# Mixture of experts over sorted token and choice pairs, in place of every expert over every token

## The reference

```python
xn = _layernorm(x)                                # (2, 1024, 128), float32
for i in range(4):                                # the transformer: 16 heads of 8
    x1 = x1 + mha(layer_norm(x1), causal mask + alibi)
    x1 = x1 + gelu(layer_norm(x1) @ ffn1.T + b) @ ffn2.T + b      # 128 -> 512 -> 128
x1 = layer_norm(x1)

logits = xf @ router_w + router_b                 # the mixture: 2048 tokens, 8 experts
top_w, sel = jax.lax.top_k(logits, 2)
gates = softmax(top_w)
for i in range(8):
    h = gelu(xf @ w1[i] + b1[i])                  # 128 -> 512
    acc += (h @ w2[i] + b2[i]) * sum(gates * (sel == i))
return x + x1 + acc
```

## Time and profile before

| | us |
|---|---|
| median of three runs | 1606.52 |
| profiled execution | 1611.84 |
| its span | 1610.0 |
| TensorE busy | 1391.6 (86% of the span) |
| VectorE busy | 1046.6 (65%) |
| ScalarE busy | 999.9 (62%) |
| GpSimd busy | 220.1 (14%) |

### The profile page before, as it was taken

One profiled execution on the slowest core, in us unless ns is written; L12 is line 12 of the kernel. 1 busy time (PEld: TensorE's weight loads), 2 busy tenths in 40 slices (PEclk: granted clock), 3 DMA queues, 4 the chain that ended last, 5 costly groups with the idle time before them and its releaser, 6 DMA issues.

```text
span 1610.0 us, 36678 instructions
## 1 busy us (share of the span) xinstructions
PE 1391.6 (86%) x12960; PEld 710.0 (44%) x12960; DVE 1046.6 (65%) x2259; ACT 999.9 (62%) x1214; POOL 220.1 (14%) x399
## 2 busy tenths in 40 slices
PE   3789898899889998798988998799998989889974
PEld 2444344454435344353443544344444535444343
DVE  5657666776676765666677766567667766676625
ACT  2055776568666775557865686565866577656841
POOL 4001200121010300112001210013001120011001
PEclk9579999999999999899999999899999999999997
DMA  5111313103021311203120130301211031201010
GB/s 184 56 29 32 97 32 99 30 30 105 24 74 32 96 32 46 75 26 97 32 74 30 30 110 20 99 17 60 82 46 58 19 97 31 78 30 31 5 47 13
DMA packets 82666, 88.87 MB, mean 55 GB/s; under 512 B 8744, under 2 KB 76080, under 8 KB 82480
## 3 DMA queue, kind: packets, MB, share of 16 engines
q1 hardware_dynamic: 82480, 86.43, 17.7%
HBM read 54.15 MB, written 33.55 MB: 54 GB/s over the span
## 4 chain that ended last, share of the span: by engine, by line
PE 67%; DVE 14%; issue 7%; ACT 7%; DMA 2%; SPq 2%; DVEq 0%; POOL 0%; ACTq 0%
PE PS L775 16%; PE PS L740 13%; PE PS L700 12%; PE PS L691 10%; DVE mx L996 7%; PE PS L757 4%; PE PS L721 2%; PE PS L745 2%; ACT PR L586 2%; PE PS L763 2%; DMA x<-orec 1%; DVE hb L920 1%; ACT hb L568 1%; PE PS L725 1%; DVE st L889 1%
## 5 line engine op out<-in xcount | busy, mean ns | idle before, releaser
L996 DVE TENSOR_REDUCE mx<-PS 128x1 f32<-128x512 f32 (+3 forms) x1280 | 773.1, 633 | 354.9 <-PE PS L745 204.1
L586 ACT ACTIVATE PR<-PS 128x1024 f32<-128x1024 f32 (+3 forms) x768 | 610.7, 808 | 441.0 <-PE PS L763 248.1
L740 PE MATMUL PS<-Kop,Qop 64*128 64x512 bf16 (+3 forms) x1536 | 415.5, 341 | 105.0 <-DVE mx L996 93.1
L757 PE MATMUL PS<-Qop,Kop 64*128 64x512 bf16 (+3 forms) x1536 | 368.3, 335 | 19.3 <-ACT PR L586 17.7
L740 PEld LDWEIGHTS PS<-Kop,Qop 64*128 64x128 bf16 x1536 | 128.4, 94 | 557.7 <-DVE mx L996 419.0
L775 PE MATMUL PS<-PR,vbuf 128*32 128x512 f32 (+3 forms) x3072 | 335.0, 509 | 0.4 <-ACT PR L586 0.4
L700 PE MATMUL PS<-wE,hb 128*128 128x128 f32 x1536 | 204.9, 284 | 14.6 <-ACT mrow L558 4.7
L700 PEld LDWEIGHTS PS<-wE,hb 128*128 128x128 f32 x1536 | 182.1, 193 | 33.6 <-issue 14.4
L745 PE MATMUL PS<-idb,mk 64*128 64x64 bf16 x2048 | 196.0, 193 | 0.0
L745 PEld LDWEIGHTS PS<-idb,mk 64*128 64x128 bf16 x2048 | 166.7, 97 | 40.7 <-issue 5.9
L763 PE MATMUL PS<-idb,mk 64*128 64x64 bf16 x2048 | 180.4, 191 | 0.0
(11 more groups left out here) (76 smaller groups left out, 940.6 us busy)
## 6 DMA issues: line engine op xcount, KB each, us to landing
Qop<-qst SPq DMA_DIRECT2D x64, 256.0 KB, 2.9
Kop<-kst SPq DMA_DIRECT2D x64, 256.0 KB, 3.2
kst<-parts SPq DMA_DIRECT2D x32, 256.0 KB, 3.0
qst<-parts SPq DMA_DIRECT2D x16, 384.0 KB, 2.8
wE<-in_moe SPq DMA_DIRECT2D x8, 514.0 KB, 3.6
kst<-parts SPq DMA_DIRECT2D x32, 128.0 KB, 2.8
qst<-parts SPq DMA_DIRECT2D x16, 256.0 KB, 2.9
Qop<-mrow SPq DMA_DIRECT2D x256, 3.0 KB
```

The lines of the kernel that those rows point to most:

```text
L586: act.activation(PR[:, c % 4, :, 0:n], PS[:, 2 * (c % 2):2 * (c % 2) + 2, 0:n], ACT.Exp)\
L740: last = pe.matmul(PS[:, 5 + k % 2, n * e:n * e + n], Qop[r, par, a, P * i:P * i + P], Kop[r, kb, a, 512 * c:512 * c + n], start=True, sto ...
L757: last = pe.matmul(PS[:, 2 * (c % 2) + j, 0:n], Kop[r, kb, a, P * kt:P * kt + P], Qop[r, par, a, q0:q0 + n], start=True, stop=not DIAG[t])
L996: dve.tensor_reduce(mx[:, par, i, 2 * heads[0] + j:2 * heads[-1] + j + 1:2, c], PS[:, 5 + k % 2, 0:n * len(heads)].rearrange("p (h n) -> p ...
```

## The change

The 4096 (token, choice) pairs are sorted by expert on the chip. Each expert's pairs fill whole tiles of 128 rows, 40 tiles in all (the most that eight experts can need), and four tiles are a group, so there are ten groups in place of 32 expert chunks.

- Before phase 0 TensorE counts, with two products of 128 x 256, how many earlier pairs go to the same expert; VectorE makes of it each pair's row (`slot`) and each tile's expert (`expert_of`), in 17 small operations spread over the first unit's first pass (`routing`). The dense gates, their transposes and the product with the second bias go. SP clears `xs` in DRAM with a DMA of 2.6 MB.
- GpSimd writes the normalised tokens into `xs` with 32 indirect DMAs of 128 rows (`scatter`): 8 and 8 in unit 0 of phase 0 and 16 in unit 1.
- For each group SP reads four expert numbers from SBUF into a register and issues nine DMAs (`group_in`): four times the expert's weights (514 KB each) and bias, and the group's rows. Before, eight DMAs of 514 KB did for the whole kernel. There is one buffer for a group.
- A group is turned (`xt`, new, four transposes), has four `h` pieces (piece f is tile f: four products of 128 x 128 with that tile's expert), a gelu and a `y`. VectorE adds the biases (for `h` with a 128 x 512 operation per piece), and SP writes the result to `ys`.
- Groups lie in unit 3 of phases 0 to 6 and in unit 2 of phases 1, 3 and 5. Unit 0 of every phase has no expert work any more, nor has unit 2 of phases 0, 2, 4, 6 and 7. All `h` of the X chunks go through ScalarE; before, VectorE did them.
- In phase 7 GpSimd gathers the rows back from `ys` with 32 indirect DMAs (16 in unit 0, 16 in unit 1), and in unit 2 multiplies by the gates and adds, in 16 operations of 128 x 512 (`combine`). The last step of the output (`final`) has three operations in place of four.

```diff
-CHUNKS = (("E", 0), ("X", 0), ("X", 1), ("E", 1), ("E", 2), ("E", 3))
-GELUS = ((0, 10), (0, 22), (1, 7), (2, 10), (2, 17), (3, 10))
+CHUNKS = (("X", 0), ("X", 1), ("E", 0), ("E", 1))
+GELUS = ((0, 22), (1, 7), (2, 11), (3, 11))
+XT_AT = {2: (2, 3), 3: (3, 3)}
...
+            def group_in(g):
+                for i in range(GROUP):
+                    e = sp.value_load(expert_of[0:1, ds(GROUP * g + i, 1)], min_val=0, max_val=E - 1)
+                    sp.dma_start(wG[:, i, :], moe[ds(e, 1), :, :].rearrange("l p n -> (l p) n")).then_inc(S["c_g"], 16)
+                    sp.dma_start(bG[:, i, :], rb_b2[ds(e + 1, 1), :].to_broadcast([P, D])).then_inc(S["c_g"], 16)
+                sp.dma_start(xG[:, :, :], xsv[ds(g, 1), :, :, :].rearrange("g p t d -> (g p) t d")).then_inc(S["c_g"], 16)
...
+                            if half == 0 and j == 2 and f is not None and b == 1:
+                                group_out(group_of(2, b, f), base + number(contents, "y", 2) + 1)
+                                group_in(group_of(3, b, f))
...
+            def scatter(first, last):
+                for k in range(first, last):
+                    pool.indirect_dma_start(out=xs[:, :], out_offset=bass.IndirectOffsetOnAxis(ap=slot[:, k:k + 1], axis=0),
+                                            in_=xe[:, k % NT, :], in_offset=None).then_inc(S["c_xs"], 16)
+            def gather(first, last):
+                for k in range(first, last):
+                    pool.indirect_dma_start(out=both[:, k // NT, k % NT, :], out_offset=None, in_=ys[:, :],
+                                            in_offset=bass.IndirectOffsetOnAxis(ap=slot[:, k:k + 1], axis=0))\
+                        .then_inc(S["c_both"], 16)
...
+                    for m in range(FT):
+                        last = pe.matmul(PS[:, bank, P * m:P * m + P], wG[:, f, P * m:P * m + P], xGT[:, P * f:P * f + P],
+                                         start=True, stop=True)
```

More of the change, by code:

```diff
@@ L172, in build @@
         rb = sb("rb", [P, E])
-        b2e = sb("b2e", [E, D])
+        tri = sb("tri", [P, P])
+        ones = sb("ones", [P, 2 * P])
+        zero = sb("zero", [P, P])
+        bound = sb("bound", [P, RANKS])
+        place = sb("place", [P, TILES])
         finw = sb("finw", [P, 2, D])
@@ L240, in build @@
         S = {n: sem(n) for n in names}
-        c_wE = [sem(f"c_wE{i}") for i in range(2)]
         c_ldl = [sem(f"c_ldl{i}") for i in range(2)]
@@ L782, in phase @@
                 row = 1 - b
-                place = f if b == 1 else q
-                g0 = 0 if f is None else gelus_before(p)
-                done = [k for k in range(6) if CHUNKS[k][0] == "E" or f is not None]
+                g0 = gelus_before(b, f)
+                done = chunks_of(b, f, q)
                 for j in range(PH):
@@ L957, in v_out, with out_of_bank @@
                                   ALU.add).then_inc(S["s_taken"], 1)
-            def out_of_bank(n, kind, which, p, biases, b, row, bank=7):
+            def out_of_bank(n, kind, which, g, biases, b, row, bank=7):
                 if kind == "h":
@@ L963, in out_of_bank @@
                 if kind == "y":
-                    y_out(n, which, p, biases, row, bank)
+                    y_out(n, which, g, biases, row, bank)
                 if kind == "wo":
@@ L1004, in maximum, with ln_step @@
                         .then_inc(S["s_negm"], 1)
-            def ln_step(idx, row, c, first, now, ready):
+            def ln_step(idx, row, c, first, now, ready, src=xr):
                 (j, k), (j0, s0) = now, first
```

407 lines of the change are left out of this document (262 added, 145 removed).

## The result

The changed kernel took 1615.85 us in the median of eight runs (1610.41 to 1619.11), the kernel before, run beside it, 1609.12. The ratio is 1.0042 with a 95% interval of 1.0022 to 1.0059: 0.4% slower, where 1550 us were predicted. The profiled execution took 1610.41 us, the one of before 1611.84; what follows compares these two, so it explains a difference of -1.4 us; by the medians it is +6.7, since the profiled execution of the changed kernel was the fastest of its eight runs.

A forecast was written before the change was run, and what follows sets the result against it. TensorE was taken to bound units with expert or transformer work, the loop of first pass and maxima the others. Savings of -116, plus GpSimd 28, SP 2 and clock 30, gave -56 us: 1550 us median, range 1515 to 1590, eight in ten 1482 to 1612.

The forecast's parts named there:

- Empty units: Six units left without expert work: 30.5 us each, five from about 41.5, unit 0 of phase 0 from 43.7; -66 us.
- Units with a group: Ten units holding an expert group: 40.4 us each, from 42.2 (seven units 3) or 41.5 (three units 2); -15 us.
- the price of a group: In each of ten units: 0.9 x 9.3 us of TensorE work on 30.5, and 1.5 for the uncovered gelu; 40.4 us.
- the term of 2 us for the groups' weights: SP loading the second group's weights in phases 1, 3, 5: 2 us in all, 15 at worst; TensorE waiting would disprove it.
- The clock: TensorE's clock halves behind 17 bare gelus, 3.8 us each: 30 us in all, bounds none and 110 us.
- Unit 0 of phases 1 to 7: Expert h ahead of the DRAM chain's end was free; only the gelu behind is saved, 2.5 of 4.5 us counted; -17 us.
- Unit 1: Half a y less in slot 0, partly covered by the X chunk's gelu: 1 us each, 2 in phase 0; -9 us.
- GpSimd: Indirect DMAs of scatter and gather make other engines wait: 28 us together, 2 us at t = 0.65, 77 at 2.13.
- t: Time one indirect DMA holds GpSimd: taken as 1.27 us, between bounds of 0.65 and 2.13.
- the stall in unit 0 of phase 7: Gather's DMAs ahead of rstd make VectorE wait in the layer norm: 20.3 - 13.7 = 6.6 us.
- rival 3: Slower, by GpSimd: its 64 indirect DMAs eat the 116 us gain at t = 2.3; 1653 us at 3.1; chance 0.12.
- rival 2: Everything is given back: clock at 60 us, GpSimd at 45, groups late by 10; 1605 us; chance 0.12.

## Why the prediction was wrong, step by step

- **Empty units: right.** 30.5 us was forecast from the stretch of the earlier trace rows; the five take 30.2 to 30.9, four of them at full clock throughout. -57 for -55. VectorE is busy for 78% of one (23.91 of 30.50 us), where over 80% was foretold.
- **Units with a group: the largest failure, 33 us.** Three terms were too small. The first is the price of a group: the model (0.9 us for each us of TensorE, 1.5 for the bare gelu) gave 40.4 us; an undisturbed one takes 41.6, so 12 us for ten. The slots show where: over an empty unit turning takes 1.6 us (0.7 in the model), the gelu 2.3 (1.5), `h` and `y` 3.5 and 3.8 (7.7 together). The second is the term of 2 us for the groups' weights, "15 at worst": the load was taken as 8 us at 326 GB/s, and ten slots, 13 us, as enough for it. It took 13.6 to 14.6 us. In phases 1, 3 and 5 TensorE waits 3.1 to 4.1 us for it, which the prediction had named as a sign that it was wrong, and then runs cold; moving the group gave 19 us in all, 15.6 in those three units. The third is the clock: 18 us were put into these units, and the extra matmuls took back 25.5, of which a part belongs to the loop's turn. How the 33 us divide among the three is not shown more closely than that.
- **The clock: right mechanism, size too small.** All 17 gelus leave TensorE idle, and behind 14 of them the clock falls (all seven of the X chunks, seven of the ten groups). 30 us were forecast, 39 were to be had behind the gelus, and 12 more behind the wait in unit 0, which the prediction had not counted at all. By its own terms: the extra matmuls took away 81 us at half clock in the units concerned, 4.8 us for each gelu where 3.8 were taken, and 35.3 us of time with it, 0.44 us for each where 0.48 were taken.
- **Unit 0 of phases 1 to 7: wrong, 19 us.** The prediction said that `h` lay beside the chain through DRAM, and that the gelu lay behind it and its 4.5 us would go, of which I counted 2.5. That step failed. The gelu did begin behind the normalise step in phases 2, 4 and 6, and ahead of it in the others; but with this work gone the normalise step starts within 0.7 us of where it did, and taking the work away alone cost 7 us. What the prediction left out is what stood in its place: the longer wait, and a clock at half for 40 us more, though it charged the clock for the 17 gelus alone.
- **Unit 1: right in sum.** +14.9 for +14: in phase 7 the gather made 9.1 of it (10.7 were forecast), in the others the fall behind the X chunk's gelu ate the shorter slot 0.
- **GpSimd: right, with luck in t.** It was taken as 1.27 us, the middle between bounds of 0.65 and 2.13, and is 1.25; nothing in the rows of before spoke for the middle. Spreading the DMAs gave 19 us against 28 forecast; the stall in unit 0 of phase 7 (6.6 us) did not show, since VectorE's wait lay there already. So rival 3, with t at 2.3 us or more, is out. The Trainium skill, "SBUF — State Buffer", section "SBUF: two separate sides", gives 3100 ns for a DMA from GpSimd beside a copy on VectorE. That did not come about here: with VectorE's maxima going on beside it, 5.2 us in the 20 us of the second half of the scatter, a DMA holds GpSimd for 1.25 us. No run shows the condition that the page names.
- **Rivals.** The outcome is rival 2, all given back, with its price of 1605 us and its causes in the main: the clock at 51 us (39 and 12; it had 60), GpSimd at 19 (45), late groups at 19 (10). It had 0.12, and the forecast 0.56, because the five sure units were set against it; they held, and the rest gave back as much. (The chance of slower, rival 3 and a quarter of rival 2, comes to 0.15 and not 0.14.)

One step was missing altogether: the loop's turn, some 6 us more than before by one execution of each kernel.

## What to carry to other kernels

When work is taken off an engine that was nearly always busy, look at each place where it goes for the wait that the work had covered: the wait stays, and the clock of TensorE falls in it. Work beside a wait or close behind it has no price of its own; what it is worth is read from a kernel with that work alone left out, not from its duration. And a transfer that can only start when a buffer comes free needs its landing time compared with the first use in the *shorter* program, not in the one whose trace lies there.

## What the runs showed of the hardware

- Matmuls that nothing reads, put where TensorE had stood idle for 2 to 7.6 us, made the program faster twice: by 39 us behind the gelus and by 12 us in unit 0.
- The same instructions with the same idle time of about 2 us kept the clock at 1.00 in one phase and not in another (unit 2 of phases 3 and 1), and which phase it is differs from run to run, so a single fall can't be forecast from the idle time alone.
- An indirect DMA of 128 rows of 512 bytes, scatter or gather, holds GpSimd for 1.25 us, with 0.30 us of issue in it.
- A turn of the loop over layers costs 9 to 10 us in the kernel before (17.8 us in the units around its two turns, 21 by the medians): TensorE stops without a semaphore for 2.3 and 2.8 us, at the first of two transfers of instructions that come 3.1 and 3.5 us apart.
